# Attention with one copy of V, and a MoE whose normalisation, router and gate search are laid over neighbouring work

## The reference, cut to what matters

```python
def _L0_xattn_ref(x, c, Wq, Wk, Wv, Wo):            # 16 heads of 64
    q, k, v = x @ Wq, c @ Wk, c @ Wv                 # split in heads
    scores = q k^T / 8, with -inf where a context row is all zero
    return (softmax(scores) @ v) @ Wo

def _L0_ffn_ref(x, gate_weight, W1, b1, W2, b2, Ws1, bs1, Ws2, bs2):
    scores = softmax(xf @ gate_weight.T).T           # 8 experts x 2048 tokens
    vals, idx = top_k(scores.reshape(-1), 2 * 2048)  # over all pairs at once
    gate = zeros at all others, vals at idx
    h = gelu(xf @ W1[e] + b1[e]);  y = h @ W2[e] + b2[e]
    out = sum_e gate[e] * y[e]
    return out + gelu(xf @ Ws1 + bs1) @ Ws2 + bs2    # the shared expert
```

## Time and profile before

| | |
|---|---|
| three runs | 2109.2, 2110.8 (median), 2112.58 us |
| profiled execution | 2111.03 us, its span 2109.3 us, so 1.7 us around the span |
| prologue of the attention, to the first subtraction | 55.6 us |
| last stage of the attention | 1492.3 to 1566 us |
| last addition of the attention ends | 1577.57 us |
| MoE, from there to its first `up` | 24.9 us |
| shared expert, first `up` to first `up` of the next | 44.5 us |
| a later expert | 22.2 us |

### The profile page before, as it was taken

One profiled execution on the slowest core, in us unless ns is written; L12 is line 12 of the kernel. 1 busy time (PEld: TensorE's weight loads), 2 busy tenths in 40 slices (PEclk: granted clock), 3 DMA queues, 4 the chain that ended last, 5 costly groups with the idle time before them and its releaser, 6 DMA issues. The chain is left out here.

```text
span 2109.3 us, 35190 instructions
## 1 busy us (share of the span) xinstructions
PE 1973.4 (94%) x10757; PEld 1444.5 (68%) x10757; DVE 1689.0 (80%) x4041; ACT 1066.2 (51%) x1494; POOL 1186.6 (56%) x646
## 2 busy tenths in 40 slices
PE   6999999999999999999999999999976899769995
PEld 4667776777677777767777777777645688557774
DVE  7888888888797888888798888888657777767755
ACT  3544545454545545453545545454534899644442
POOL 4655665657575665757575666657764445224340
PEclk8999999999999999999999999999986999879997
DMA  3000000000000000000000000000000212112210
GB/s 96 1 1 17 1 3 17 1 2 3 18 1 3 1 16 1 4 18 1 1 4 17 1 3 1 1 1 1 1 9 13 92 60 80 37 47 63 80 30 24
DMA packets 56397, 40.76 MB, mean 19 GB/s; under 512 B 2516, under 2 KB 53660, under 8 KB 55196
## 3 DMA queue, kind: packets, MB, share of 16 engines
q1 hardware_dynamic: 56220, 38.57, 6.1%
HBM read 37.45 MB, written 1.11 MB: 18 GB/s over the span
## 5 line engine op out<-in xcount | busy, mean ns | idle before, releaser
L479 POOL TENSOR_TENSOR a_den<-a_den,a_probs 128x1024 f32<-128x1024 f32 x352 | 845.7, 2404 | 344.4 <-ACT a_probs L695 343.3
L695 ACT ACTIVATE a_probs<-a_probs,a_mask_col 128x1024 f32<-128x1024 f32 x416 | 478.8, 1151 | 585.8 <-DVE a_probs L890 585.6
L890 DVE TENSOR_TENSOR a_probs<-a_scores,a_shift 128x512 f32<-128x512 f32 x832 | 565.8, 686 | 155.6 <-PE a_scores L508 134.1
L826 DVE CUSTOM_DVE_ANT_0 a_work<-a_work,a_mask_row 128x400 f32<-128x400 f32 (+1 forms) x1024 | 572.2, 590 | 47.2 <-PE a_work L540 47.0
L593 PE MATMUL a_pv<-a_probs,a_V 128*64 128x256 f32 x3328 | 406.8, 387 | 0.9 <-ACT a_probs L695 0.9
L506 PE MATMUL a_scores<-a_Q_hi,a_cT_hi 128*128 128x512 f32 x832 | 345.7, 416 | 6.9 <-DVE a_probs L890 5.0
L507 PE MATMUL a_scores<-a_Q_lo,a_cT_hi 128*128 128x512 f32 x832 | 328.3, 395 | 0.0
L508 PE MATMUL a_scores<-a_Q_hi,a_cT_lo 128*128 128x512 f32 x832 | 326.7, 393 | 0.8 <-issue 0.7
L540 PE MATMUL a_work<-a_cT_hi,a_Q_hi 128*128 128x400 f32 (+1 forms) x1024 | 323.4, 363 | 2.9 <-DVE a_maxes L826 1.9
L593 PEld LDWEIGHTS a_pv<-a_probs,a_V 128*64 128x64 f32 x3328 | 221.0, 137 | 150.1 <-issue 41.0
L540 PEld LDWEIGHTS a_work<-a_cT_hi,a_Q_hi 128*128 128x128 f32 x1024 | 191.5, 188 | 98.3 <-issue 44.2
(11 more groups left out here) (334 smaller groups left out, 2855.9 us busy)
## 6 DMA issues: line engine op xcount, KB each, us to landing
m_gate_rows<-gate_scratch SPq DMA_DIRECT2D x8, 1024.0 KB, 4.5
a_c_nat<-in_ctx_dram SPq DMA_DIRECT2D x8, 768.0 KB
b_c_in<-in_ctx_dram SPq DMA_DIRECT2D x8, 768.0 KB
b_c_nat<-in_ctx_dram SPq DMA_DIRECT2D x8, 768.0 KB
m_w_raw<-in_L_ffn_W_dram SPq DMA_DIRECT2D x16, 256.0 KB, 4.8
a_acc<-in_x_dram SPq DMA_DIRECT2D x8, 128.0 KB, 2.1
out_dram<-tokens SPq DMA_DIRECT2D x4, 256.0 KB, 2.3
tokens<-in_x_dram SPq DMA_DIRECT2D x1, 896.0 KB, 9.6
```

Source lines behind the costliest of these rows:

```text
L479: nc.gpsimd.tensor_tensor(half, so_far, probs[:, buffer(c, j), :], ALU.add).then_inc(den_added, 1)
L695: nc.scalar.activation(probs[:, buffer(c, j), :], probs[:, buffer(c, j), :], ACT.Exp, bias=mask_col[:, c // 2 % 2, chunk:chunk + 1]).then_ ...
L826: nc.vector.tensor_tensor_reduce(out=X[:, bank, :w], in0=X[:, bank, :w], in1=mask_row[:, off:off + w], scale=1.0, scalar=-3e38, op0=ALU.ad ...
L890: nc.vector.tensor_tensor(probs[:, buffer(c, j), pair * 2 * S:(pair + 1) * 2 * S], Sc[:, pair, :], shift[:, first:first + 2 * S], ALU.add) ...
```

## The change

It has four parts.

1. V has one copy. Chunks 0 to 3 of the next stage are made at the end of a stage (slots 95 to 102, when they have been used), chunks 4 to 12 of a stage in that stage itself. So the last stage, which had none, now makes nine; TensorE waits at each chunk for its eviction.
2. The prologue: raw weights lie in `probs` and `shift`; GpSimd's split of Wv waits until the four flags of the context are there; only seven chunks of V and two of the four Q items are left in it, and the rest goes to the first slots of stage 0.
3. In the last stage of the attention lie now the MoE's small weights, the statistics of 14 tiles (two groups of seven, slots 14 to 28), their scaling (14 instructions, slots 46 to 75), transposes (`mT`), router logits (`ml`), and on GpSimd the split of the shared expert's weights.
4. In `moe_0` the first `up` waits for none of that; the last two tiles follow after steps 0 to 2. The 15 rounds are spread over 22 steps of the shared expert and expert 1 (`ROUND_AT` 5, 6, 8, 9, ... 24, 26), ties at step 28, gates at 29. GpSimd cuts the first 24 steps. Expert 1's output is kept as `raw_y` and multiplied by its gates during expert 2.

```diff
+            pool.wait_ge(flag_done, 4)
...
+            for n, i in enumerate(range(FIRST_VS, NC)):
+                slots[1 + 2 * n].append((-1, "v", i))
...
+                slots[n] += [(c - 1, "v", i) if kind == "own_v" else (c, kind, i) for kind, i in slot]
+        else:
+            for i in range(EARLY_V, NC):
+                slots[1 + 2 * (i - EARLY_V)].append((c - 1, "v", i))
         if c == STAGES - 1:
 
+            slots[10].append((STAGES, "mw", 0))
+            for g in range(2):
+                for n, kind in enumerate(("sum", "centre", "square", "var")):
+                    slots[14 + 8 * g + 2 * n].append((STAGES, kind, g))
+            slots[44].append((STAGES, "rstd", 0))
+            for t, slot in enumerate((46, 47, 48, 49, 50, 51, 53, 54, 65, 67, 69, 71, 73, 75)):
+                slots[slot].append((STAGES, "scale", t))
+            for g, slot in enumerate((52, 57, 74, 80)):
+                slots[slot].append((STAGES, "mT", g))
+            for g, slot in enumerate((59, 63, 82, 86)):
+                slots[slot].append((STAGES, "ml", g))
...
+                    if half == 0:
+                        taken(pe, it, v_use(it, c, chunk))
...
+                elif kind == "scale":
+                    if i >= 8 and i % 4 == 0:
+                        filled(dve, None, use_of(the_plan(None, STAGES - 1), STAGES, "mT", i // 4 - 2))
+                    nc.vector.tensor_scalar(m_xn(i), XS[:, i, :], stats[:, 0, i:i + 1], stats[:, 1, i:i + 1],
+                                            ALU.subtract, ALU.mult).then_inc(m_scaled, 1)
...
+    ROUND_AT = [5 + 3 * r // 2 for r in range(ROUNDS)]
+    TIES, GATES = ROUND_AT[-1] + 2, ROUND_AT[-1] + 3
+    POOL_CUTS = STEPS + 8
...
-            load_weights(0, ws1, ws2)
             load_weights(1, w1[0, :, :], w2[0, :, :])
             sp.wait_ge(gateT_done, 1)
             sp.dma_start(gate_dram, gateT[:, :]).then_inc(gate_stored, 16)
...
-                sp.wait_ge(w_split, at(it, 8, 4 * c))
+                if c > 1:
+                    sp.wait_ge(w_split, at(it, 8, 4 * c - 4))
                 e = at(it, 2, c)
                 load_weights(c + 1, w1[e, :, :], w2[e, :, :])
...
+                if g in ROUND_AT:
+                    pe.wait_ge(counted, 3 * (ROUND_AT.index(g) + 1))
...
-                if k == 0:
-                    pe.wait_ge(w_split, at(it, 8, 4 * c + 4))
+                if k == 0 and c > 0:
+                    pe.wait_ge(w_split, at(it, 8, 4 * c))
...
+                    if it is None and g == POOL_CUTS:
+                        dve.wait_ge(lo_done, POOL_CUTS)
```

More of the change, by code:

```diff
@@ L137, in prep_slots @@
         early += [("q", i) for i in range(4)]
-        vs = [("v", c) for c in range(NC)]
+        own = [("own_v", i) for i in range(EARLY_V, NC)]
         for u in range(UNITS * 4):
             early.append(("max", u))
-            if u in V_AFTER:
-                early.append(vs.pop(0))
+            if u in V_AFTER and with_own:
+                early.append(own.pop(0))
         slots = [[] for _ in range(SLOTS)]
@@ L151, in prep_slots @@
             slots[SPREAD[i]].append(("spread", i))
-        assert len(vs) == len(LATE_V)
-        for n, item in zip(LATE_V, vs):
-            slots[n].append(item)
+        for i in range(EARLY_V):
+            slots[LATE_V[i]].append(("v", i))
         return slots
     CONTEXT_ITEMS = 4
-    PREP = [sum(map(len, prep_slots(g))) - 4 for g in range(2)]
     SPLIT = (0, STAGES - 1)
-    MOVED = 34
     STD_STEP, SCALE_STEP = 4, 8
+    FIRST_VS = 7
     def where(c, j):
@@ L171, in adds_with, with takes_bank, raw_plan @@
         return j + 1 if j < 2 else j - 1
[L173 to L195 removed]
+    def takes_bank(kind):
+        return kind not in ("recip", "shift", "diag", "sum", "centre", "square", "var", "rstd", "scale")
+    def raw_plan(c, tail, prep):
         slots = [[] for _ in range(SLOTS)]
@@ L584, in pv @@
                         pe.wait_ge(pv_free, at(it, 8, 2 * c - 1 + half))
-                    if chunk == NC - BANKS and half == 0:
-                        for use in range(first_use(c) - BANKS, first_use(c)):
-                            taken(pe, it, use)
+                    if half == 0:
+                        taken(pe, it, v_use(it, c, chunk))
                 for odd in range(2):
@@ L1029, in experts @@
         def experts(eng, body):
-            body(None, 0)
-            body(None, 1)
-            with eng.Fori(0, E // 2 - 1) as it:
-                for c in (2, 3):
+            for c in range(4):
+                body(None, c)
+            with eng.Fori(0, E // 2 - 2) as it:
+                for c in (4, 5):
                     body(it, c)
@@ L1083, in body @@
                     sp.wait_ge(y_taken, at(it, 2 * TG, c * TG))
+                if it is None and c == 2:
+                    sp.wait_ge(raw_scaled, TG)
                 load_gate(c + 1, e)
-            body(None, 1)
-            with sp.Fori(0, E // 2 - 1) as it:
-                for c in (2, 3):
+            for c in (1, 2, 3):
+                body(None, c)
+            with sp.Fori(0, E // 2 - 2) as it:
+                for c in (4, 5):
                     body(it, c)
@@ L1264, in _ @@
-            for g in range(4):
-                cols = slice(g * 512, (g + 1) * 512)
-                dve.wait_ge(xT_hi_done, g + 1)
-                nc.vector.tensor_tensor(xT[1][:, cols], U[:, g, :], f32(xT[0][:, cols]), ALU.subtract)\
-                  .then_inc(xT_done, 1)
+            mean, var = stats[:, 0, :], stats[:, 1, :]
+            link(nc.vector.tensor_reduce(mean, XS[:, LATE, :], AX.X, ALU.add))
+            link(nc.vector.tensor_scalar(mean, mean, 1.0 / D, None, ALU.mult))
+            link(nc.vector.tensor_tensor(xn[:, :, :], XS[:, LATE, :], bc(mean, D), ALU.subtract))
```

416 lines of the change are left out of this document (274 added, 142 removed).

## The result

| | before | after |
|---|---|---|
| median of seven runs each | 2110.8 us | 2123.47 us (2118.67 to 2126.55) |
| ratio, after to before | | 1.0055, 95% interval 1.0041 to 1.0069 |
| the profiled execution's span | 2109.3 us | 2124.4 us |

The changed kernel is slower, by 0.0055 x 2110.8 = 11.6 us. The profiled execution of the changed kernel is the slowest of its seven (2126.55 us), so its pieces are held against those of the other kernels too. The page after, as in the earlier trace rows: as many TensorE instructions at a lower share.

A forecast was written before the change was run, and what follows sets the result against it. TensorE, busy 94% of the span, was taken to bound the kernel. Last stage +19, MoE -7.6 and prologue -6 summed to +5.4 on 2110.8, giving 2116.2 us, range 2100 to 2126 (own range 2112 to 2121).

The forecast's parts named there:

- much slower: Rival, chance 0.15: in the search, one-step rounds lose GpSimd's lock race, a pair takes 6.6 us, total 2123 us.
- prologue: first subtraction earlier: Prologue: flags no longer delayed and Q and V items moved out bring the first subtraction 9.7 us earlier, at about 46.
- what stage 0 takes back: First slots of stage 0: moved Q and V items cost 5.6 us, a third falling into idle time, so 3.7.
- (a): Last attention stage: nine V chunks are 6.3 us of TensorE, of which idle time takes 2.6, so +3.7 us.
- (b): Last attention stage, slots 14 to 28: statistics on VectorE, with waits for GpSimd, add +7.7 us.
- (c): Last attention stage: fourteen scalings on VectorE, each possibly waiting for GpSimd, mostly covered by idle, +2.6 us (0 to 8).
- (d): Last attention stage: 14 transposes and 42 router logits on TensorE at full clock, +5 us (3 to 8).
- 14 gaps between rounds: Search in the MoE: six pairs of rounds at 5.4 us plus two last gaps, together 39.8 us (36 to 46).
- clock and `raw_y` in expert 2: Expert 2: slower clock after the idle costs 2.5 us, scaling `raw_y` costs 1.
- MoE gain: MoE: expert 2 starts 82.9 us after E instead of 91.6; less 1 for `raw_y`, gain 7.6 us (3 to 14).
- the prediction's rule: VectorE two-port copies or scalings, or instructions with two SBUF inputs, wait for whole GpSimd instructions; reductions never; decides 13 or 19.
- the growth: Sign of being wrong, last attention stage: growth below 14 us, where +19 (10 to 27) was forecast.

The follow-up runs named there:

- e2: The changed kernel with the statistics of the 14 tiles left out of the last attention stage: 2112.02 us, ratio 0.9997 to the kernel before.
- e1: The changed kernel with expert 2's weight load issued ahead of SyncE's wait for the gates: 2111.96 us, ratio 0.9999 to the kernel before.
- f1: The kernel of e1 with the search's running threshold kept in PSUM in place of SBUF: 2108.83 us, ratio 0.9984 to the kernel before the change.
- f2: The changed kernel without GpSimd's wait for the four flags ahead of its split of Wv: 2126.78 us, ratio 1.0065 to the kernel before.
- g3: The changed kernel with the last stage's nine V chunks made with one matmul in place of three: 2120.03 us, ratio 1.0040 to the kernel before.
- e3: The changed kernel with the statistics at slots 28 to 42 in place of 14 to 28: 2115.4 us, ratio 1.0015 to the kernel before.
- e4: The changed kernel with the 14 scalings on ScalarE in place of VectorE: 2120.35 us, ratio 1.0044 to the kernel before.
- f4: The changed kernel with the edits of e1, e3 and e4 together: 2107.4 us, ratio 0.9973 to the kernel before.
- g2: The changed kernel with expert 2's weights early, threshold in PSUM, `raw_y` spread, and statistics three slots apart (26 to 47): 2104.83 us, ratio 0.9965 to before.

## Why the prediction was right, step by step

The prediction said slower, 2116.2 us in 2100 to 2126; 2123.5 is inside, 7 above its value. Its own range for the forecast was 2112 to 2121, and the time lies outside that. It lies where the rival "much slower" had put it (2121 to 2133), but not by that rival's mechanism: a pair of rounds would have had to take over 6 us, and six pairs took 5.3 in the mean. So the direction and the mechanisms were those of the forecast, and its size was too small in one place, the last stage. E is the end of the attention's last addition. The last stage is counted from the V product ahead of the V chunks to E: 1577.57 - 1488.66 = 88.91 before, 1596.14 - 1480.83 = 115.31 after. The terms:

| term | predicted | measured | from |
|---|---|---|---|
| prologue: first subtraction earlier | 9.7 | 7.8 | 55.60 to 47.76 |
| what stage 0 takes back | 3.7 | 1.1 | -7.8 to -6.7 |
| last stage (a), V | +3.7 | +5.4 | first piece without statistics (e2), 24.21 - 18.76 |
| (b), statistics | +7.7 | +11.6 | 98.03 - 86.46 |
| (c), (d) | +7.6 | +10.3 | third piece without statistics (e2), 49.32 - 39.04 |
| end | | -0.9 | behind the V product near the end |
| last stage | +19 | +26.4 | sum |
| first round after E | 19 | 17.9 | 1614.02 - 1596.14 |
| 14 gaps between rounds | 39.8 | 39.8 | 1653.80 - 1614.02 |
| last round to store | 9.1 | 8.7 | 1662.54 - 1653.80 |
| store to expert 2 | 12.5 | 12.6 | 1675.12 - 1662.54 |
| clock and `raw_y` in expert 2 | 3.5 | 4.3 | 26.86 - 22.52 |
| MoE gain | 7.6 | 8.0 | 113.8 - 105.8, at expert 3 |

The last row: expert 3 began at 1669.2 + 22.2 = 1691.4, 113.8 after E, and begins at 1701.98, 105.8 after E. The sum of the terms is 26.4 - 6.7 - 8.0 = 11.7, beside 11.6 by the ratio. That they agree so closely is in part luck, since the one profiled pair differs by 15.1. Behind the last `up` of the last expert, where the code is the same, the changed kernel took 3.9 us more in that execution, with a mean clock of 0.70 against 0.79 in the 41 us from the first transposition of the last attention's context on; over all fourteen traces this stretch takes 284.9 to 289.9 us (before 285.9, changed 289.8). The other experts took 0.7 more, and stages 1 to 14 together 1.1 less. The end, -0.9, is no effect of the change either: behind the V product near the end the traces show 18.17 or 17.28 us, and both occur with the same code.

**MoE** was right in its path, the 10 us of idle ahead of expert 2 above all (10.26), and e1 shows its cause: the same idle is gone with one line moved. The price of `raw_y` (3.5 in e1, where the clock is full) was put at 1, and the clock's at 2.5. In this pair 0.8 is left for the clock; over the traces expert 2 takes 25.6 to 26.9 us with the gap ahead of it and 25.8 to 26.4 without, so no price of the clock can be told there. Only the sum of the two was near. As to the rounds, the total of 39.8 was hit by two errors that cancel: the first six pairs took 31.5 us (5.1, 4.9, 6.2, 5.1, 5.1, 5.1) where 32.4 had been said, and the last two gaps, with VectorE cutting, 8.25 where 7.4 had been said. f1 shows the reason given for a pair above 4.7, waits for GpSimd; it gained 3.2 us.

**The prologue** was right in cause. f2 shows that the wait for the flags brings 3.8 us of the first maximum's 28.55 - 24.07 = 4.5, where 5.2 had been said. The Q and V items that left take 3.3 to 4.5 us off the way from the first maximum to the first subtraction in the thirteen traces after the change (4.5 had been said). What stage 0 takes back was put too high: 0.6 to 1.5 in the same traces, where 3.7 had been said.

**The last stage** is where the size was off, in each of its terms. (a) let 2.6 of V's 6.3 us "take" TensorE's idle. The step that failed is that the idle of a whole stage was offered to slots that don't have it: in the same piece before, TensorE was busy 18.13 of 18.76, so it had 0.6 to give. Without the statistics V costs 5.4, and g3 agrees, with 3.1 of 4.2 us.

(b) The twelve instructions took 14.6 us on VectorE, 8.9 of work (the prediction: 9.3) and 5.7 of waits for GpSimd (the prediction: 3.7, in four waits of the large ones). The large ones lost 2.6, in two waits. What it left out is that the four tiny multiplications wait as well: two of them alone lost 1.86 + 1.47 - 2 x 0.17 = 3.0 us. It then hid half of the waits in idle time that the work had used up. And it counted no slower clock here, only for expert 2; about 3.1 us of the second piece are that. The two reductions of each group took 1.02 to 1.08 us in every kernel, so on this the prediction's rule held. e2 shows that the term is real, e3 that its place makes more than half of it. (The prediction's own figures, 5.7 and half of 3.7, make 7.55 and not 7.7.)

(c) and (d) were put at 7.6 and are 10.3. TensorE's added work was right (5.9 said, 5.7 more busy in the third piece). e4 takes 3.8 us off with the scalings on ScalarE, more than all of (c), 2.6; in f4, with the statistics later, the same edit takes off nothing. How the rest splits stays open.

Of the signs of being wrong that the prediction named, the growth (26.4) and the idle (10.26) are as said. The third, that no stage from 1 to 14 changes by more than 0.2, failed in two: stage 5 is 1.7 us shorter and stage 9 is 1.1 longer. Both are differences of the granted clock over the same work (last section), and the other stages differ by less than 0.15. That the chunks at the end of a stage cost nothing is thus borne out.

What was not tried: the changed kernel without any V in its last stage, since its data are needed there, and an attention that leaves the transposes and logits to the MoE.

## What to carry to other kernels

Offer the idle time of an engine only to the slots where it lies: a stage that is 4% idle may have none where the work goes. When a result comes later than before, look through the DMA queue for loads that stand behind it without needing it; here one such load cost 12 us, as much as the change had lost. An instruction of 128x7 elements is not free beside GpSimd: ask of each where its operands lie, and read its longest time from a trace. Those that someone waits for can go to ScalarE, or get an operand in PSUM, which was tried here for the merges of the search alone. The same waits cost less away from slots that VectorE already fills (16.0 us on VectorE in e3, 14.6 in the changed kernel, and a last stage 6.2 us shorter), and more where TensorE's clock falls behind them, as in g2.

## What the hardware showed that was not expected

TensorE's clock also falls where both kernels do the same work, in one execution and not in the other. The same stretch of stage 5, before, and in the changed kernel:

```profile
546.20:557.30 11.10, 11.10 (x65) 7.52 (x64) 9.41 (x18) 4.42 (x7) 4.79 (x2) 0.85 0.27 76
```

```profile
539.20:548.64 9.44, 9.44 (x65) 6.93 (x64) 9.08 (x18) 4.45 (x7) 4.80 (x2) 1.00 0.32 89
```

The granted clock was 0.85 and 1.00, and the stretch took 11.10 and 9.44 us, with TensorE busy throughout in both. Stage 9 shows the reverse, 0.91 in the changed kernel and 1.00 before. Such a dip of 1 to 2 us is as large as some effects here, so that a single trace says where a microsecond went, and not whether it comes again.
